# Layer 1's last 24 pairs as one stacked fp16 matmul, with a reordered weight setup and gathers signalled in four groups

## What is computed

```python
e = jnp.stack([tbl_f[ids[:, f]] for f in range(48)], axis=1)      # 512 x 48 x 32

def _cin_layer(xi, x0, W, b):
    Fi, F0 = (xi.shape[1], x0.shape[1])
    Wr = W.reshape(Fi, F0, -1)
    out = jnp.einsum('nie,nje,ijo->noe', xi, x0, Wr) + b[None, :, None]
    return jax.nn.relu(out)

xs = [e]                                # three layers, 128 outputs each
for W, b in ((W1, b1), (W2, b2), (W3, b3)):
    xs.append(_cin_layer(xs[-1], e, W, b))
z = jnp.concatenate(xs, axis=1).sum(axis=-1)
h = jnp.concatenate([z, dense_ctx], axis=1)
h = jnp.maximum(h @ W_top1 + b_top1, 0.0)
h = jnp.maximum(h @ W_top2 + b_top2, 0.0)
y = h @ W_top3
```

## Time and profile before

| | us |
|---|---|
| median of three runs | 2486.8 |
| lowest and highest run | 2486.18, 2488.17 |
| the profiled execution | 2486.23 |
| its span | 2484.4 |
| TensorE busy (share of the span) | 2388.0 (96%) |
| VectorE busy | 2208.1 (89%) |
| ScalarE busy | 1976.3 (80%) |
| GpSimd busy | 2018.3 (81%) |

### The profile page before, as it was taken

How to read it: one execution, slowest core, us unless ns; L and a number is a source line. 1 busy time by engine, 2 the same in 40 slices (tenths; PEclk the granted TensorE clock), 3 DMA queues, 4 the chain that set the end, 5 groups by cost and what they waited for, 6 DMA issues and landing times.

```text
span 2484.4 us, 66691 instructions
## 1 busy us (share of the span) xinstructions
PE 2388.0 (96%) x13149; PEld 1326.8 (53%) x13149; DVE 2208.1 (89%) x9242; ACT 1976.3 (80%) x7182; POOL 2018.3 (81%) x2009
## 2 busy tenths in 40 slices
PE   1599999999999999999999999999999999999998
PEld 0355555555555555555555555555555555555553
DVE  4399999999999999999999999999999999999995
ACT  1388888888888888888888888888888888888874
POOL 7488888888878888888778888888877777777773
PEclk6799999999999999999999999999999999999999
DMA  4000000000000000000000000000000000000000
GB/s 165 9 12 12 11 10 11 11 11 9 9 10 11 11 11 11 12 11 10 9 9 11 11 10 11 11 11 11 9 10 9 9 8 9 10 9 9 9 10 3
DMA packets 113450, 34.35 MB, mean 14 GB/s; under 512 B 107860, under 2 KB 111575, under 8 KB 113400
## 3 DMA queue, kind: packets, MB, share of 16 engines
q1 hardware_dynamic: 107256, 30.73, 5.3%
q0 software_dynamic: 6144, 3.16, 0.8%
HBM read 12.82 MB, written 0.00 MB: 5 GB/s over the span
## 4 chain that ended last, share of the span: by engine, by line
PE 94%; DVE 1%; issue 0%; DMA 0%; ACT 0%; SPq 0%; DVEq 0%
PE y L411 79%; PE m L401 11%; PE m L392 3%; DVE acc L672 1%; PE m L466 0%; PE y L473 0%; PE y L466 0%; DMA xT<-lo 0%; DVE ends L672 0%; PE y L479 0%; DVE msum L681 0%; DVE ends L686 0%; DVE pooled L725 0%; SPq L249 0%; DVE acc L668 0%
## 5 line engine op out<-in xcount | busy, mean ns | idle before, releaser
L411 PE MATMUL y<-whi,xT 128*128 128x512 f16 x6144 | 1990.7, 379 | 11.2 <-DMA xT<-lo 8.1
L503 ACT ACTIVATE work<-y,xc 128x128 f32<-128x128 f32 x5632 | 1611.3, 372 | 394.5 <-PE y L411 367.0
L672 DVE SCALAR_TENSOR_TENSOR acc<-y,xc,acc 128x128 f32<-128x128 f32 x5632 | 1669.4, 342 | 83.4 <-PE y L411 78.4
L311 POOL TENSOR_TENSOR part<-part,work 128x512 f32<-128x512 f32 x896 | 1137.5, 1270 | 214.9 <-ACT work L503 132.8
L411 PE MATMUL y<-wlo,xT 128*128 128x512 f16 x3072 | 1165.3, 379 | 0.0
L411 PEld LDWEIGHTS y<-whi,xT 128*128 128x128 f16 x6144 | 601.3, 98 | 623.8 <-issue 10.2
L401 PEld LDWEIGHTS m<-wsq,work 128*128 128x128 f32 x2560 | 388.6, 193 | 93.9 <-ACT work L523 1.9
L411 PEld LDWEIGHTS y<-wlo,xT 128*128 128x128 f16 x3072 | 300.9, 98 | 249.9 <-issue 0.8
L401 PE MATMUL m<-wsq,work 128*128 128x128 f32 x2560 | 391.2, 276 | 1.1 <-ACT work L523 1.1
L307 POOL TENSOR_TENSOR part<-work 128x512 f32<-128x512 f32 x256 | 326.6, 1276 | 62.2 <-ACT work L503 57.7
L272 POOL DMA_INDIRECT emb<-tbl,ids_sb x192 | 196.8, 1025 | 44.3 <-issue 26.6
(11 more groups left out here) (81 smaller groups left out, 958.1 us busy)
## 6 DMA issues: line engine op xcount, KB each, us to landing
xT<-hi SPq DMA_TRANSPOSE x256, 2.2
xT<-lo SPq DMA_TRANSPOSE x256, 2.4
emb<-tbl,ids_sb POOLq DMA_INDIRECT x192, 2.4
xx<-w SPq DMA_DIRECT2D x4, 768.0 KB, 8.9
work<-w SPq DMA_DIRECT2D x4, 768.0 KB, 15.0
x0T<-x0hl SPq DMA_TRANSPOSE x128
wt_sb<-W_top SPq DMA_DIRECT2D x1, 768.0 KB
w1s<-w_pair SPq DMA_DIRECT2D x1, 640.0 KB
```

The source lines that it names most:

```text
L311: pool.tensor_tensor(a[:], a[:], p[:, m, :], ALU.add).then_inc(s, 1)
L411: ins = nc.tensor.matmul(dst[:], xT[layer][:, parity, a, :], w[layer][:, cols], start=i == 0, stop=i == 2)
L503: nc.scalar.activation(prods[layer][:, a, k * P:(k + 1) * P], bank[:, k * P:(k + 1) * P], ACT.Copy, scale=xc[layer][:, parity, j:j + 1]).t ...
L672: ins = nc.vector.scalar_tensor_tensor(dst, y, col, mine, ALU.mult, ALU.add)
```

## The change

**Stacked matmul.** The last group of layer 1 has 24 pairs (REST). Its pair sums are now formed three times, at rows 0, 32 and 64 of the group (COPIES; the matrix `sel` and the weights are copied on the host). ScalarE squares the 88 rows (STACK) twice, rounded to fp16 into `zst` and in fp32 into free columns of the same PSUM bank; VectorE subtracts the rounded squares from the fp32 ones in rows 32 to 55, so `zst` holds hi, lo, hi. `wst` holds the weights as hi, hi, lo. One fp16 matmul with 88 rows then replaces one of the ten fp32 matmuls of a tile. So that squares and weights suit fp16, `wsq` is divided by a power of two of its own, squares are scaled by SQUARE, and `msq`, which scales the result back, takes a second small ScalarE operation every second step. The second and third pair sums and squares move from n = 16 and 20 to n = 14 and 17; the subtraction stands at n = 22 of VectorE, and TensorE's layer 1 waits for it.

**Setup.** SyncE loads the eight pieces of w2 and w3 ahead of the small weights. The three matmuls and the VectorE chain for winv come first, those for wsq after. ScalarE writes the weights, scaled, into the five y banks in 24 pieces of 512 columns, and VectorE forms `wlo` as bank minus `whi`, piece by piece, each bank being free again after its piece. The clearing of `pooled` moves from GpSimd to VectorE.

**Gathers.** The first 48 gathers signal four semaphores, 12 each, and VectorE spreads a group into `xx` when it has landed.

```diff
+REST = PAIRS - (KT - 1) * P
+COPIES = (0, 32, 64)
+STACK = COPIES[-1] + REST
...
-SETUP = 6
+GATHERS, SPREAD, GROUP = 2, 8, 12
+W1_SETUP = 7
+SETUP = W1_SETUP + 2 * BANKS
 PAIR_BANK = (1, 0, 0)
-PAIRS_AT = (12, 16, 20)
+PAIRS_AT = (12, 14, 17)
...
+SQUARE = 2.0 ** -8
...
             sp.dma_start(ids_sb[:], ids.rearrange("(b p) f -> p b f", p=P)).then_inc(s_ids, 16)
+            for l, w in enumerate((w2, w3)):
+                for c in range(4):
+                    n = F * P // 4
+                    sp.dma_start(raw[l][:, c * n:(c + 1) * n], w[:, c * n:(c + 1) * n]).then_inc(s_w[l][c], 16)
             sp.dma_start(w1s[:], w_pair).then_inc(s_in, 16)
             sp.dma_start(w1b[:], w_pair_t).then_inc(s_in, 16)
             sp.dma_start(sel[:], select).then_inc(s_in, 16)
             sp.dma_start(member[:], pairs_of).then_inc(s_in, 16)
             for l in range(3):
                 sp.dma_start(brow[:, l * P:(l + 1) * P], b_cin[l].rearrange("(a n) -> a n", a=1)).then_inc(s_in, 16)
-            for l, w in enumerate((w2, w3)):
-                for c in range(4):
-                    n = F * P // 4
-                    sp.dma_start(raw[l][:, c * n:(c + 1) * n], w[:, c * n:(c + 1) * n]).then_inc(s_w[l][c], 16)
...
-            gather(0, range(F))
-            for l in range(3):
-                pool.memset(pooled[:, :, l, :], 0.0).then_inc(s_pool[l], 1)
+            for f, landed in zip(range(0, F, GROUP), s_first):
+                gather(0, range(f, f + GROUP), landed)
...
             pe.wait_ge(s_const, 5)
+            pe.wait_ge(s_wchain, 9)
+            nc.tensor.transpose(misc[0][0:1, 0:P], wmax[:, 8:9], eye32[:]).then_inc(s_wpe, 1)
+            pe.wait_ge(s_wchain, 12)
+            nc.tensor.matmul(misc[0][:, 0:1], ones[:], wmaxr[:, 2:3], start=True, stop=True).then_inc(s_wpe, 1)
             pe.wait_ge(s_in, 7 * 16)
             nc.tensor.matmul(misc[1][:, 0:3 * P], ones[:], brow[:], start=True, stop=True).then_inc(s_wpe, 1)
+            pe.wait_ge(s_wchain, 13)
             pe.wait_ge(s_setup, 1)
             for k in range(KT):
                 ins = nc.tensor.matmul(misc[0][0:F, 0:P], member[:, k, :], w1s[:, k, :], start=k == 0, stop=k == KT - 1)
             ins.then_inc(s_wpe, 1)
-
-            pe.wait_ge(s_wchain, 9)
-            nc.tensor.transpose(misc[0][0:1, 0:P], wmax[:, 8:9], eye32[:]).then_inc(s_wpe, 1)
-            pe.wait_ge(s_wchain, 12)
-            nc.tensor.matmul(misc[0][:, 0:1], ones[:], wmaxr[:, 2:3], start=True, stop=True).then_inc(s_wpe, 1)
+            pe.wait_ge(s_wchain, 15)
+            nc.tensor.transpose(misc[1][0:1, 0:P], wmax[:, 9:10], eye32[:]).then_inc(s_wpe, 1)
+            pe.wait_ge(s_wchain, 18)
+            nc.tensor.matmul(misc[1][:, 0:1], ones[:], wmaxr[:, 5:6], start=True, stop=True).then_inc(s_wpe, 1)
...
                 if c == 0:
                     wait(pe, s_zts, t * 3 + 3)
+                    wait(pe, s_zst, t + 1)
                 for k in (2 * c, 2 * c + 1):
-                    ins = nc.tensor.matmul(misc[0][:, 0:P], zT[:, k, :], wsq[:, k, :], start=k == 0, stop=k == KT - 1)
+                    z, w = (zT[:, k, :], wsq[:, k, :]) if k < KT - 1 else (zst[0:STACK, :], wst[0:STACK, :])
+                    ins = nc.tensor.matmul(misc[0][:, 0:P], z, w, start=k == 0, stop=k == KT - 1)
...
                 nc.scalar.activation(whi[l][:], raw[l], ACT.Copy, scale=winv[:, 0:1]).then_inc(s_split, 1)
+                for n in range(BANKS):
+                    i = l * BANKS + n
+                    if i >= RING:
+                        act.wait_ge(s_setup, W1_SETUP + i - RING + 1)
+                    nc.scalar.activation(ybank[i % RING][:], raw[l][:, n * Q * P:(n + 1) * Q * P], ACT.Copy,
+                                         scale=winv[:, 0:1]).then_inc(s_scaled, 1)
...
-                nc.scalar.activation(msq[:], mp0[:], ACT.Square).then_inc(s_msq, 2)
+                nc.scalar.activation(mpsq[:], mp0[:], ACT.Square).then_inc(s_mpsq, 2)
+                wait(act, s_mpsq, t + 2)
+                nc.scalar.activation(msq[:], mpsq[:], ACT.Copy, scale=zunit[:]).then_inc(s_msq, 2)
             def square_pairs(t, g):
                 wait(act, s_zt, t * 3 + g + 1)
                 if g == 0:
                     wait(act, s_l1, t)
-                n = min(4, KT - 4 * g)
+                n = min(4, KT - 1 - 4 * g)
+                if g == 2:
+                    rest = misc[PAIR_BANK[g]][0:STACK, n * P:(n + 1) * P]
+                    nc.scalar.activation(zst[0:STACK, :], rest, ACT.Square, scale=SQUARE)
+                    nc.scalar.activation(misc[PAIR_BANK[g]][0:STACK, (n + 1) * P:(n + 2) * P], rest, ACT.Square,
+                                         scale=SQUARE)
                 nc.scalar.activation(zT[:, 4 * g:4 * g + n, :].rearrange("p t c -> p (t c)"),
-                                     misc[PAIR_BANK[g]][:, 0:n * P], ACT.Square).then_inc(s_zts, 1)
+                                     misc[PAIR_BANK[g]][:, 0:n * P], ACT.Square, scale=SQUARE).then_inc(s_zts, 1)
...
-            for l in range(2):
-                dve.wait_ge(s_split, l + 1)
-                nc.vector.scalar_tensor_tensor(wlo[l][:], raw[l], winv[:, 0:1], whi[l][:], ALU.mult,
-                                               ALU.subtract).then_inc(s_setup, 1)
...
+            nc.vector.tensor_scalar(wsq[:], wsq[:], winv[:, 1:2], None, ALU.mult).then_inc(s_setup, 1)
+            dve.wait_ge(s_setup, 5)
+            nc.vector.tensor_copy(wst[:], wsq[:, KT - 1, :]).then_inc(s_setup, 1)
+            dve.wait_ge(s_setup, 6)
+            rows = slice(COPIES[2], COPIES[2] + REST)
+            nc.vector.tensor_tensor(wst[rows, :], wsq[rows, KT - 1, :], wst[rows, :], ALU.subtract).then_inc(s_setup, 1)
+            for i in range(2 * BANKS):
+                l, n = i // BANKS, i % BANKS
+                cols = slice(n * Q * P, (n + 1) * Q * P)
+                dve.wait_ge(s_scaled, i + 1)
+                nc.vector.tensor_tensor(wlo[l][:, cols], ybank[i % RING][:], whi[l][:, cols],
+                                        ALU.subtract).then_inc(s_setup, 1)
+            def spread(g, e0, e1):
+                fields = slice(g * GROUP, (g + 1) * GROUP)
+                return nc.vector.tensor_copy(xx[:, e0:e1, fields], emb[:, 0, fields, e0:e1].rearrange("p f e -> p e f"))
+            for g in range(F // GROUP - 1):
+                dve.wait_ge(s_first[g], 16 * GROUP)
+                spread(g, 0, E)
+            dve.wait_ge(s_first[F // GROUP - 1], 16 * GROUP)
             for e0, e1 in ((0, 4), (4, E)):
-                nc.vector.tensor_copy(xx[:, e0:e1, :], emb[:, 0, :, e0:e1].rearrange("p f e -> p e f")).then_inc(
-                    s_xx, e1 - e0)
+                spread(F // GROUP - 1, e0, e1).then_inc(s_xx, e1 - e0)
...
+            def stacked_lo(t):
+                rows = slice(COPIES[1], COPIES[1] + REST)
+                wait(dve, s_zts, t * 3 + 3)
+                nc.vector.tensor_tensor(zst[rows, :], misc[0][rows, 2 * P:3 * P], zst[rows, :],
+                                        ALU.subtract).then_inc(s_zst, 1)
...
+                        if n == 22 and k == 0 and active(t1 + 1):
+                            stacked_lo(t1 + 1)
...
+    def copied(a):
+        for c in COPIES[1:]:
+            a[Z - P + c:Z - P + c + REST] = a[Z - P:Z - P + REST]
+        return a
```

74 lines of the change are left out of this document (48 added, 26 removed).

## The result

The changed kernel takes **2481.8 us** (median of 19 runs, 2462.3 to 2486.4), the one before 2487.4 in the same session (2485.8 to 2488.8): the ratio is 0.9964, 95% interval [0.9949, 0.9978]. It is 0.4% faster, where 1.2% was forecast (2456.9 us), and it lies outside the range of 2452 to 2467. Its runs spread over 24 us, those of the kernel before over 3. The profiled execution took 2483.2 us around its span of 2481.3.

A forecast was written before the change was run, and what follows sets the result against it. TensorE's successive matmuls were taken to bound the loop, GpSimd's gathers the start. Terms -9.5, -1.1, +0.4, +0.6 and -20.3 summed to -29.9 us, giving 2456.9 us from 2486.8; range 2452 to 2467.

The forecast's parts named there:

- The setup, costed at nothing: Before the loop: the longer weight setup would end by 63.9, before the last gather at 67.0; cost nothing, cover 3 us.
- Rival D: Start: setup ends after the gathers, later than 67 us, each us costing one; at 3 us, 2460; chance 0.06.
- The gathers (-9.5): Start: two gathers no longer blocked by wide VectorE operations, 10.8 us, less 1.3 for new operations beside gathers; net -9.5 us.
- the last group (-1.1): Start: after the last row lands only a quarter of the old 1.61 us copy remains, some 0.5 us; -1.1 us.
- rival A: Start: VectorE's subtraction from PSUM blocks the gathers all the same, so the 10.8 us stay; 2466.4 us, chance 0.09.
- The first tiles (+0.4 and +0.6): First tile and tile 2: layer 1 starts later, behind extra squares and VectorE's subtraction; +0.4 us and +0.6 us.
- All terms of the start together: Everything before the steady loop, gathers, last group and first tiles: 9.6 us gained.
- The step (-20.3): Loop: one fp32 matmul (0.222 us) becomes one fp16 matmul (0.057), saving 0.165 us in each of 123 steps; -20.3 us.
- the margin of 0.4 us: Loop: VectorE's subtraction ends at about 828.9, and TensorE wants it at 829.27 for layer 1; so no wait.
- VectorE's lateness: Loop: lo comes 0.5 us later with hi, absorbed by 0.70 us of VectorE's existing waits for TensorE; costed at nothing.
- lo was to wait for hi longer: Loop, a sign expected in the changed profile: VectorE's lo waits longer for ScalarE's hi, which comes about 0.5 us later.
- Rival C: Loop: layer 1 waits for the subtraction in each step, stall 0.45 us if squares take twice their slot; 2512 us, chance 0.04.

The follow-up runs named there:

- the squares first: Changed kernel with small loads, membership matmuls and the squares' weight chain put back ahead of the large weights' maxima, rest of the change kept: 2460.9 us, ratio 0.9893.
- the kernel with the third group in the other bank: Kernel with the squares first, third pair-sum group moved to the other PSUM bank, so only layer 1's last, stacked matmul waits for the subtraction: 2456.6 us, ratio 0.9878.

## Why the prediction was wrong

- **The setup, costed at nothing with "its cover is 3 us or more": this step failed.** The sum of the work under it was right: with the squares first the setup ends at 62.7 against a bound of 63.9, and the gathers bound the start. What was left out is when VectorE and TensorE exchange signals: the membership matmuls and the correction stood at 11 to 15 us in the kernel before, the two round trips for the new scale did not exist, and all three now come when the bulk loads end or later. The profile of the kernel before showed each of its signals arriving at once, so no row there could give the 11 to 31 us of the first signal, nor the further 0 to 4 of each of the next two. Rival D, that the setup ends after the gathers, is what happened, though it named none of this. It had 0.06, with 3 us as its example; it was 22 (89.5 against 67).
- **The gathers (-9.5) and the last group (-1.1) were right.** The first reduction comes at 67.04 in the kernel with the squares first, 11.1 us earlier than before where 10.6 was forecast; rival A is false, since no gather beside the 24 pieces of that kernel takes more than 0.95 us. One reading under the -9.5 was incomplete: the gather of 9.68 (2.16 us) would have been over at 10.63, before L594 begins at 10.89, so the addition ahead of it (L592, from 9.37 for 1.49 us, both operands in SBUF) must have held it first.
- **The first tiles (+0.4 and +0.6) were somewhat low.** From the first reduction to the piece of 21 matmuls (137.50 in the kernel before) it was 59.3 us in the kernel before and 61.2 with the squares first: 1.9 instead of 1.0. The two waits of TensorE for the subtraction, 1.1 and 1.4 us, stand where layer 1 waited 0.47 and 0.62 us for ScalarE's squares before, so they are some 1.4 us of it. All terms of the start together gave -9.25 there (128.25 against 137.50) where -9.6 was forecast.
- **The step (-20.3) was mis-sized by a fifth, not in the matmul but in its wait.** The stacked matmul costs the 0.057 us that the forecast took from the pair sum. The sentence that failed is the margin of 0.4 us between subtraction and layer 1: in every second step there is none, and TensorE loses 0.05 us. By the 81 ns of the Trainium skill ("TensorE: Matmul & The Clock Gate", Back-to-back issue gap) the period would be 18.189, an estimate, and near the 18.195 measured; the kernel with the third group in the other bank, at 18.168 with the same matmul, shows that the likeness is an accident.
- **Apart from that wait VectorE's lateness was covered**: its waits for acc's bank fell from 78.4 to 50.0 us over the kernel, and with the wait gone the period is 18.168, so nobody on TensorE paid for it. But one of the signs named for it is wrong: lo was to wait for hi longer, and these waits fell from 46.0 to 29.3 us. Rival C is false.
- **The range** left out the one case in which the start goes wrong by more than 10 us. Its own bounds were also added up loosely: with the -15.3 and -20.3 of the step they give 2455 to 2464, and the -27.3 named as a limit, which would give 2448, was not used. The number itself, 2456.9, comes out as 2456.6 in a kernel with another order of the setup and without the step's wait; some luck is in that, since there the first tiles cost more than forecast and the gathers gave more.

## What to carry to other kernels

When a change moves a chain of engine-to-engine signals to another time, costing its instructions is not enough: ask what else runs at the new time, and what happens if one signal in it is late by tens of us. Here a cover of 3 us was none; putting the chain early, or one added wait that moved it clear of the end of the bulk loads, gave back over 20 us. When the runs of a kernel spread over 24 us where its predecessor's spread over 3, ask for a wait that is not work: here it stood as "remote" in the waits, a single one of 33 us.
